# Low halves, residual and bias sums on GpSimd, key variance from a gram product in token layout, and another order of stages, in a two-layer transformer kernel

## The reference, cut to what matters

```python
xn = layernorm(x)
x = x + L0_attn(xn) + L0_ffn(xn)      # 16 heads of 16; feed-forward 704 wide, silu gate
xn = layernorm(x)
x = x + L1_attn(xn) + L1_experts(xn)  # experts: 32 of 96 plus a shared one of 192, top 6 by router
# L1_attn, per head (16 inputs per head, latent 64):
c = xh @ Wdkv.T; c = (c - mean(c)) * rsqrt(var(c) + 1e-5) * ln_g + ln_b
scores = (xh @ absorbed) @ c.T / 8;  v = c @ Wuv   # causal softmax, then two output products
```

## Time and profile before

| | us |
|---|---|
| median of 3 runs (range) | 2845.7 (2838.66 to 2846.57) |
| the profiled execution: its own time, its span | 2846.51, 2844.9 |
| TensorE matmuls busy (share of the span) | 1996.1 (70%) |
| VectorE busy | 1390.0 (49%) |
| ScalarE busy | 808.5 (28%) |
| GpSimd busy | 368.6 (13%) |

### The profile page before, as it was taken

How to read it: one execution, slowest core, us unless ns; L and a number is a source line. 1 busy time by engine, 2 the same in 40 slices (tenths; PEclk the granted TensorE clock), 3 DMA queues, 4 the chain that set the end, 5 groups by cost and what they waited for, 6 DMA issues and landing times.

```text
span 2844.9 us, 48024 instructions
## 1 busy us (share of the span) xinstructions
PE 1996.1 (70%) x15632; PEld 1321.9 (46%) x15632; DVE 1390.0 (49%) x4438; ACT 808.5 (28%) x1581; POOL 368.6 (13%) x412
## 2 busy tenths in 40 slices
PE   3257958577695866859576785867769576775958
PEld 1124635345363544536444463544446354453636
DVE  2535446363554536445363544536355453635543
ACT  1322423223142232313223241322324223231413
POOL 1001101011111101111020110102111020111112
PEclk9957969879697887969788797978879688797969
DMA  2704031140402214040130404013040311404030
GB/s 60 167 13 90 3 83 21 35 72 16 89 2 67 39 27 79 12 92 4 49 58 16 90 4 92 11 37 70 16 90 3 77 28 27 79 14 91 2 75 5
DMA packets 318528, 135.64 MB, mean 48 GB/s; under 512 B 224784, under 2 KB 305744, under 8 KB 318288
## 3 DMA queue, kind: packets, MB, share of 16 engines
q1 hardware_dynamic: 302928, 82.05, 13.8%
q0 software_dynamic: 15360, 50.34, 9.3%
HBM read 102.12 MB, written 29.88 MB: 46 GB/s over the span
## 4 chain that ended last, share of the span: by engine, by line
issue 47%; DMA 15%; PE 12%; POOL 12%; DVE 7%; SPq 5%; ACT 2%; POOLq 0%; DVEq 0%; ACTq 0%
POOL gs L554 9%; DMA cb<-comb_d 8%; SPq L452 3%; POOL cb L549 3%; PE s1b L1096 2%; DMA part_d<-part 2%; PE s1acc L1096 2%; DMA xn<-o_d 2%; PE s2acc L1093 1%; PE s1a L1096 1%; PE s2r L1096 1%; DMA comb_d<-ct 1%; DVE st L766 1%; SPq L487 1%; PE s2r L1102 1%
## 5 line engine op out<-in xcount | busy, mean ns | idle before, releaser
L554 POOL TENSOR_TENSOR gs<-gs,cb 128x512 f32<-128x512 f32 x192 | 245.0, 1276 | 1376.5 <-DVE gs L985 1147.9
L1096 PE MATMUL s3r<-part,xu 128*128 128x256 f16 x2304 | 319.0, 294 | 84.2 <-DVE th L995 84.2
L1096 PE MATMUL s3r<-part,xg 128*128 128x256 f16 x2304 | 327.3, 299 | 0.0
L1093 PE MATMUL s2acc<-xd,h2h 128*128 128x256 f16 x1536 | 287.7, 289 | 36.0 <-DVE h2l L976 36.0
L1096 PEld LDWEIGHTS s3r<-part,xu 128*128 128x128 f16 x2304 | 241.7, 106 | 135.0 <-DVE th L995 91.7
L718 ACT CAST h2h<-th 128x512 f16<-128x512 f32 (+1 forms) x224 | 131.4, 587 | 586.0 <-DVE th L995 556.8
L1096 PEld LDWEIGHTS s3r<-part,xg 128*128 128x128 f16 x2304 | 238.4, 106 | 62.5 <-issue 20.1
L549 POOL DMA_DIRECT2D cb<-comb_d x192 | 111.1, 586 | 1090.0 <-DMA comb_d<-ct 896.1
L995 DVE TENSOR_TENSOR th<-s3r,gs 128x512 f32<-128x512 f32 x192 | 131.7, 686 | 216.3 <-POOL gs L554 216.3
L985 DVE SCALAR_TENSOR_TENSOR gs<-th,s3r 128x512 f32<-128x512 f32 (+1 forms) x224 | 144.1, 643 | 185.1 <-ACT th L714 184.7
L1093 PE MATMUL s2acc<-xd,h2l 128*128 128x256 f16 x768 | 223.0, 290 | 0.0
(11 more groups left out here) (284 smaller groups left out, 3223.4 us busy)
## 6 DMA issues: line engine op xcount, KB each, us to landing
cb<-comb_d POOLq DMA_DIRECT2D x192, 256.0 KB, 10.6
part_d<-part SPq DMA_DIRECT2D x32, 512.0 KB, 3.3
va<-v_d SPq DMA_DIRECT2D x512, 8.0 KB
land<-part_d SPq DMA_DIRECT2D x96, 64.0 KB, 2.8
part<-part_d SPq DMA_DIRECT2D x96, 64.0 KB, 10.5
qst<-part_d SPq DMA_DIRECT2D x96, 64.0 KB, 2.3
kst<-part_d SPq DMA_DIRECT2D x96, 64.0 KB, 2.3
x<-in_L_attn_x SPq DMA_DIRECT2D x16, 256.0 KB, 3.7
```

The source lines that it names most:

```text
L554: g.tensor_tensor(gc2[:, p % 2, :], gs2[:, p % 2, :], cb2[:, 2 * p:2 * p + 2, :].rearrange("p a s -> p (a s)"), ALU.mult).then_inc(sem("gc ...
L1093: ins = nc.tensor.matmul(bk, lhs[i][k], rhs[j][k], start=first and chain[0], stop=last and chain[1], skip_group_check=True)
L1096: ins = nc.tensor.matmul(bk, lhs[i][k], rhs[j][k], start=first, stop=last)
```

## The change

`h1l`, `h2l`, `y1` (layer 0's residual sum), `xb2` (x2 plus output bias) and the addition of `val_const` to the values move from VectorE to GpSimd, which gets streams `gp1`, `gp2`, `gp3` and the same string as the others. The DMAs of `cb2` are issued in b's stage qr0, behind `xb2` and the `h1l` of f0 to f2. The gram product is made with tokens on the partitions, like the values, and multiplied with `xn2`; a VectorE reduction over 16 channels takes the place of the product with `head_mean8`; `x2f` is no longer made. `TURNS` is another.

```diff
-TURNS = [int(c) for c in ("100011212220001111111211221020212020110220102102121021202202"
-                         "0220010200002022222202")]
+TURNS = [int(c) for c in ("101102210020011111121210122122012020121020120121212010220202"
+                         "0202000000210222222022")]
-U2 = ["x", "gram", "var_t", "k", "v", ...
+U2 = ["x", "gram", "k", "v", ...
+        def gp1(gp, it):
+            def low(c):
+                gp.wait_ge(*event("h1h_made", it, c + 1))
+                gp.wait_ge(*event("down1_done", it, c - 1))
+                g.tensor_tensor(h1l[0:m, c % 2, :], h1[0:m, c % 2, :], h1h[0:m, c % 2, :], ALU.subtract)
+            ...                        # low(c) in stages f0 .. f5, then in kr0:
+            g.tensor_tensor(y1[:, :, :], gs1[:, :, :], x1[:, :, :], ALU.add)
+        def gp2(gp, it):
+            ...                        # stage comb:
+            g.tensor_tensor(xb2[:, :, :], x2[:, :, :], bo_row..., ALU.add)
+            yield
+            gp.wait_ge(*event("comb_saved", it, 16))
+            ...                        # the 12 DMAs of cb2
+            for t in range(T):
+                g.tensor_tensor(va2[:, t, :, 0:HD], va2[:, t, :, 0:HD], val_const..., ALU.add)
+        def gp3(gp, it):
+            for n in range(UNITS):
+                if n >= 2:
+                    ...                # wait for cb2 once, then
+                    g.tensor_tensor(gc2[:, p % 2, :], gs2[:, p % 2, :], cb2[...], ALU.mult)
+                yield
+                gp.wait_ge(*event("h2h_made", it, n + 1))
+                gp.wait_ge(*event("down2_done", it, n - 1))
+                g.tensor_tensor(h2l[0:m, n % 2, 0:w], th2[0:m, n % 2, 0:w], h2h[0:m, n % 2, 0:w], ALU.subtract)
+                yield
-            s.copy(x2f[:, :, :], two(bk)).then_inc(sem("x2_parts"), 1)
-            v.tensor_tensor(pr2[:, :, :], two(bk), x2f[:, :, :], ALU.mult)
-            v.tensor_scalar(rt2[:, :, :], bk[:, 0:T * H]..., 0.0, EPS, ALU.max, ALU.add)
+            v.tensor_tensor(pr2[:, :, :], two(bk), xn2[:, :, :], ALU.mult)
+            v.tensor_reduce(rt2[:, :, :], pr2[:, :, :].rearrange("p t (h d) -> p t h d", d=HD), AX.X, ALU.add)
+            v.tensor_scalar(rt2[:, :, :], rt2[:, :, :], 0.0, L * EPS, ALU.max, ALU.add)
-            for k in range(K):
-                ins = parts3(two(bk)[:, k, :], [[f[:, k, 2, :]] for f in fold], [[x[:, k, :]] for x in x2p])
-            ...                        # wait, then 4 products with head_mean8
             for t in range(T):
                 for k in range(K):
+                    ins = parts3(two(bk)[:, t, P * k:P * k + P], [[x[k]] for x in xt[t]], [[f[:, k, 2, :]] for f in fold])
```

More of the change, by code:

```diff
@@ L309, in program @@
         pairs2 = [[("k_rows", n), ("k_rows", n + 1)] for n in range(0, H, 2)]
-        U2 = numbered(["x", "gram", "var_t", "k", "v", "logit", "rs", "comb"] + [("q_rows", n) for n in range(H)] + ["max"]
+        U2 = numbered(["x", "gram", "k", "v", "logit", "rs", "comb"] + [("q_rows", n) for n in range(H)] + ["max"]
                       + pairs2[0] + pairs2[1] + pairs2[2] + [("pv", 0)] + pairs2[3] + pairs2[4] + [("pv", 1)] + pairs2[5] + pairs2[6]
@@ L549, in gp3 @@
                     gp.dma_start(dst, src[(4 * i + q) // 3].partition_broadcast(32)).then_inc(sem("cb2_loaded"), 16)
[L550 to L555, removed]
+            gp.wait_ge(*emptied2(it, U2["v"]))
+            for t in range(T):
+                g.tensor_tensor(va2[:, t, :, 0:HD], va2[:, t, :, 0:HD], val_const[:, :].rearrange("p (h d) -> p h d", h=H),
+                                ALU.add).then_inc(sem("va2_made"), 1)
+            yield
+            for n in range(HG):
+                yield
+            for n in range(HG):
+                yield
+            yield
+        def gp3(gp, it):
+            g = nc.gpsimd
+            for n in range(UNITS):
+                m, w = unit(n)
+                if n >= 2:
+                    p = n - 2
+                    if p == 0:
+                        gp.wait_ge(*event("cb2_loaded", it, 16 * 12))
+                    gp.wait_ge(*emptied3(it, n, 0))
+                    g.tensor_tensor(gc2[:, p % 2, :], gs2[:, p % 2, :],
+                                    cb2[:, 2 * p:2 * p + 2, :].rearrange("p a s -> p (a s)"), ALU.mult).then_inc(sem("gc2_made"), 1)
+                yield
+                gp.wait_ge(*event("h2h_made", it, n + 1))
+                gp.wait_ge(*event("down2_done", it, n - 1))
+                g.tensor_tensor(h2l[0:m, n % 2, 0:w], th2[0:m, n % 2, 0:w], h2h[0:m, n % 2, 0:w], ALU.subtract).then_inc(sem("h2l_made"), 1)
+                yield
+            yield
         @block.gpsimd
@@ L587, in _ @@
                     g.memset(r[:, :, j, :], vals[j]).then_inc(sem("rows_made"), 1)
-            with gp.Fori(0, B) as it:
-                gp3(gp, it)
+            run(None, gp1(gp, 0), None)
+            with gp.Fori(1, B) as it:
+                run(gp2(gp, Before(it)), gp1(gp, it), gp3(gp, Before(it)))
+            run(gp2(gp, B - 1), None, gp3(gp, B - 1))
         def root(act, it, mv, name):
@@ L882, in dve2 @@
             bk = ring2[U2["gram"] % 2]
[L883 to L886, removed]
+            v.tensor_tensor(pr2[:, :, :], two(bk), xn2[:, :, :], ALU.mult).then_inc(empties2(U2["gram"]), 1)
+            dve.wait_ge(*emptied2(it, U2["gram"]))
+            v.tensor_reduce(rt2[:, :, :], pr2[:, :, :].rearrange("p t (h d) -> p t h d", d=HD), AX.X, ALU.add).then_inc(sem("var2_summed"), 1)
+            dve.wait_ge(*event("var2_summed", it, 1))
+            v.tensor_scalar(rt2[:, :, :], rt2[:, :, :], 0.0, L * EPS, ALU.max, ALU.add).then_inc(sem("var2_made"), 1)
             yield
@@ L970, in dve3 @@
             v = nc.vector
[L972 to L976, removed]
             for n in range(UNITS):
@@ L997, in dve3 @@
                 yield
-            low(UNITS - 1)
             yield
```

60 lines of the change are left out of this document (31 added, 29 removed), and 2 rows, old and new, of the table PER.

## The result

The changed kernel takes 2741.1 us (median of 2737.97, 2741.05 and 2747.51) against 2844.9 for the kernel before in the same series: ratio 0.9643 [0.9615, 0.9671], 3.6% faster. A fourth run took 3790.05 us, in the slow state, and is left out. The profiled execution took 2747.51 us with a span of 2745.7; before it was 2846.51 and 2844.9, so 99 us are to be explained from the two traces.

What follows compares the result with a forecast made beforehand. Bound by the chain through `part2`, loads and `cb2` for a turn's first 70 us, then TensorE. Per turn -0.2 -2.2 -0.4 +0.7 = -2.1, times 15 is -31.5, last pass -1: from 2846.5 to 2814 us; range 2750 to 2860.

Steps and rivals of the forecast that it cites:

- the first part: From the turn's start through variance and router: `part2` ends 6.0 us earlier, the loads start 4.6 us earlier.
- 2.2 of clock: Behind D2's start TensorE is already back at full speed: 2.2 us less per turn, bounds 0 and 2.6.
- 0.4 of VectorE's relief: From 1122 to 1166, handing `h2l` to GpSimd gives back 0.4 us per turn, bounds 0 and 2.4.
- no wait for h2l except before D13: Sign of being right: TensorE waits for `h2l` only before D13, there 0.6 us longer than the 2.23 before.
- D2's start: First down product of a routed unit: at 1116.9, 0.2 us earlier, in the turn starting at 1046.2.
- From its landing ... Sum 12.6: D2 at 1116.9: From `land1`'s landing at 1104.3, copies, heads, max, D1, gate, up and b:kr0 take 12.6 us until D2.
- the two heads 2.5: Between the copies to `kst1` and max: the two heads of a:qr0 take 2.5 us on the way to D2.
- The 1 us for the store of `v_d`: The store falls into the DMA engines' busy time and delays `cb2` and `land1` by 1 us.
- the forecast's case: VectorE waits for `land1`, and behind it TensorE with max, D1, G3 and then D2: 2814 us, chance 0.50.
- land1 lands first: Rival: `land1` lands before `cb2`, D2 follows `cb2` by 5.5 us: -3.6 to -6.6 per turn, about 2775; chance 0.25.
- The new wait costs more than it saves: Rival: SyncE's head start is eaten, `land1` lands at 1107.9, D2 3.4 us later: turn 1.5 longer, 2869; chance 0.13.
- Nothing comes of it: Rival: gaps in the products between `land1` and D2 keep the clock low: +0.1 us per turn, 2848; chance 0.12.

Runs made afterwards that it cites:

- wait_scores: The changed kernel with a TensorE wait added behind the two heads of a:qr0 for VectorE's maxima of these heads: 2779.3 us, 0.9779.
- vd_later: The changed kernel with the store of `v_d` moved behind the 12 loads of `land1` in SyncE's queue: 2726.8 us, 0.9568.
- all_dve: The kernel before with the new string and new variance path, all elementwise work still on VectorE: 2739.3 us, 0.9620.
- old_order: The changed kernel with the string of stages of the kernel before: 2804.2 us, 0.9855.
- split_h2l_qr0: The changed kernel with `h2l` back on VectorE, `cb2` in 24 half-size DMAs, first-used half first, and a:qr0 behind b:kr0: 2669.1 us, 0.9387.
- order_alone: The kernel before with only the new string of stages: 2823.0 us, 0.9925.

## Why the prediction was right or wrong

*Right: the first part.* `part2` was to end 18.8 us after the turn's start and ended at 18.7; the reduction took 0.69 us (0.7 taken); the loads were to be issued at 24.3 and were at 24.3 in the mean. The router's wait was to shrink to about 2 us and did (33.4 over 16). The direct way from gram to the loads was well read.

*Right: behind D2.* From D2 to a:kr0 the forecast was 2.6 less (2.2 of clock, 0.4 of VectorE's relief), measured 1.9; from a:kr0 on 0.7 more, measured 0.9. Full clock stands directly behind D2. TensorE's waits for `h2l` sum to 49.6 us over 35, of which the one ahead of D13 makes 36.8 (2.45 in each of 15 turns, 2.8 foreseen). The sign "no wait for h2l except before D13" held in substance only: D12 waits 0.2 in each turn, and in three turns D1 waits 2.0 to 2.6, hidden in the wait for `cb2`. The copies to `kst1` met `gc2` as assumed, in the eleven turns: in the shown one four took 2.63 us in place of 1.53. The rule of the Trainium skill (SBUF — State Buffer, Who interferes with whom) agrees here: such a copy waits for the rest of a GpSimd instruction, 1516 less 421 ns being below the 1268 of one.

*Failed: D2's start.* It was forecast at 71.0 us (1116.9), 0.2 earlier than in the turn that was read, and came at 65.7 in the mean: 5.3 us a turn, 79 over 15. (The turn that was read has its D2 0.4 later than the mean of before, so as a change of the means 73 were missed.) This 79 has three parts of like size.

The first, 29 us, is the sum "From its landing ... Sum 12.6: D2 at 1116.9". In the eleven turns in which `land1` lands with `cb2`, D2 follows it by 10.0 us in the mean. The term "the two heads 2.5" is the mistake: it is VectorE's time for the maxima of a:qr0, and I put it on TensorE's path between the copies and max. TensorE issues these scores, does not wait for their maxima, and goes on: its max transposes need only layer 1's maxima, long done. From the first score to max it is 0.54 us. All the other terms together take 10.2 us in the shown turn, where the prediction has 10.1, and 9.4 in the mean. wait_scores builds the wait in: the shown chain grows to 12.3, and the time by 22 (profiled) to 38 us (medians).

The second, 25 us, is the landing of `land1`, forecast at 58.4 and measured at 56.1 in those turns (`cb2`: 58.8 and 55.6). The issue of `cb2` came 0.5 us earlier than forecast. The length of the burst, which I took as fixed, is 1.2 us less: from the first issue to the landing of `cb2` it was 22.8 us in these turns before and 21.6 after. About 0.6 stays unexplained. The 1 us for the store of `v_d` was sized about right (0.7 to 1.0 in vd_later).

The third, 25 us, is that the forecast's case was taken for all turns. In four it was the rival's, and D2 came at 64.7.

That the time missed by 67 us only (2747.5 against 2814) is the balance of 73 at D2, 4.9 ahead of the loop and 2.7 in the last pass, less 10 from D2 to a:kr0 and 3 behind it, where the gain was smaller than forecast.

*Half right: the rival "land1 lands first".* Its mechanism and its size hold where it works. In the first turn (`land1` at 44, `cb2` at 57, D2 at 62.0) and in three others (49 to 50, 60 to 61, D2 at 65.6) D2 follows `cb2` by 5.2 us in the mean (5.5 forecast), and comes 8.0 earlier than in the same turns before. Its condition is not the rule, and its reason was another than the one given: in the three turns GpSimd's queue pauses in the midst of its issues, and does so before the change too. In the other eleven turns D2 gained 4.0, not the 0.2 of the forecast's own case. The two cases are not rivals but mix in one run; the range, cut at 2750, followed from taking them as apart.

*The other rivals.* "The new wait costs more than it saves" fell: it hung on a landing above 1106.4, which is 60.5 after the start, and it came at 56.1. "Nothing comes of it" fell with the clock.

*Outside the sum.* Ahead of the loop 4.9 us went where 0 was expected; the last pass lost 3.7 where 1 was. The sum has no term for the loads ahead of the loop.

So the gain is that of the variance path and the order, and of both together; the work on GpSimd, the largest part of the diff, is worth nothing on the whole (all_dve 2739.3, changed kernel 2741.1). Part of the variance path's share, the burst and the loads ahead of the loop, came by luck: it was in nobody's sum, and its cause is open.

## What to carry to other kernels

Before a duration is put into a chain, read which engine waits for it: an instruction between two others in time lies on the path only if someone waits for its result, and building the supposed wait into a kernel shows it in one run. Where two transfers end together, whatever waits behind them hardly gains from reordering; sending first the half that is needed first took GpSimd's wait from 188 us to 6 and gave 36 us, where moving some 370 us of small operations to an idle engine gave nothing. A mean over the turns of a loop can hide two kinds of turns, each bound by another transfer; read more than one turn before you choose the chain. Two parts that each shorten one chain are tested in a square of four kernels, since a hop counts only when nothing covers it.

## What the runs showed of the hardware

- GpSimd's queue pauses in the midst of the 12 DMAs of `cb2`, in the third, eighth and thirteenth turn of the loop: six are issued, then none for 9.6 to 13.0 us, then the other six. These are the same three places (behind the 30th, 90th and 150th of 192) in all ten kernels with 12 DMAs, the one before among them. `land1` then lands well ahead of `cb2`: in the changed kernel at 49 to 50, and `cb2` at 60 to 61. With 24 DMAs of half the size the longest pause within a turn is 1.2 us. The profile names nothing that the queue waits for. The third turn of the changed kernel:

```profile
554.90 3.49 POOL L584 DMA_DIRECT2D cb<-comb_d  x6 [1.30 <-DMA comb_d<-ct]
570.34 4.02 POOL L584 DMA_DIRECT2D cb<-comb_d  x6 [11.94 <-issue]
```

- Which of two bursts lands first followed their head start. With 1.8 us between the first issues of `land1` and `cb2` both land at 56 (changed kernel, eleven turns); with 4.1 us (old_order) `land1` lands at 48.9 and `cb2` at 60.1.
- From the first issue of `cb2` to its last landing, in the same eleven turns, 3.9 MB are moved in 22.8 and 23.1 us in the two kernels with the old variance path (168 to 170 GB/s), and in 21.2 to 21.7 us in the six with the new one and the same transfers (180 to 183 GB/s). The kernels differ in `x2f` and `head_mean8`, which are gone, and so perhaps in where their other tiles lie; no run here isolates the cause.
- The same broadcast as 24 DMAs of half the size (split_h2l_qr0, against the changed kernel) kept its cost of issue per DMA, 552 ns against 586, and a DMA landed in 6.9 us in the median against 9.8: nearly twice the issue time on GpSimd, yet a wait for `cb2` of only 1.7 us over the span.
- A low half of 128x512 on GpSimd, f32 operand and f16 operand to f16, took 1156 ns (median), the f32 product of the same shape 1268 (mean).
- The weights' loads ahead of the loop go with the variance path too. In the stretch 80:100 both kernels with the old path (before, order_alone) move 261 GB/s, and their loop starts at 205.2 and 204.3; the eleven with the new one move 311 to 333 GB/s, and start at 197.4 to 200.8. Why is not shown. The stretch in the kernel before, then after:

```profile
80.00:100.00 20.00, 0.00 (x0) 0.00 (x0) 10.55 (x6) 9.90 (x7) 0.00 (x0) 1.00 1.27 261
```

```profile
80.00:100.00 20.00, 0.00 (x0) 0.00 (x0) 13.53 (x8) 12.47 (x9) 0.00 (x0) 1.00 1.15 333
```
